# One graph-attention layer: the attention stage in 64-row matmuls, two side by side

## The chip, the core and the metric

The kernel runs on one core of a Trainium2 chip. Its time is the device time in microseconds (us) of that core; of several runs the median counts. In the profile PE is TensorE's matmul side and PEld its weight loads, DVE is VectorE, ACT is ScalarE, POOL is GpSimd and SP is SyncE, which here issues most of the DMAs.

## What is computed

A graph layer over 384 nodes with 1024 features, 16 heads of 64, and a mask from 6528 typed edges. All matrices are 1024 x 1024 in float32.

```python
h = relu(layernorm(x))
q, k, v = h @ wq.T + bq, h @ wk.T + bk, h @ wv.T + bv
q2, k2, v2 = q @ wiq.T + biq, k @ wik.T + bik, v @ wiv.T + biv   # then split into 16 heads of 64
scores = einsum('hnd,hmd->hnm', q2, k2) * 0.125 + mask           # mask from the edges, 384 x 384
out = einsum('hnm,hmd->hnd', softmax(scores), v2)
return x + out @ wo.T + bo
```

## The kernel before, in words

Every factor of a matmul is split into a high part (rounded to the matmul's format) and a low part (the remainder), and a product is three matmuls: high x high, low x high, high x low (`products`, L882 to L886). The high part of anything is made by ScalarE, the low part by VectorE or GpSimd, each behind the other.

The weights come as 56 slabs of 128 x 1024 (512 KB), numbered in the order of use: 0 to 7 v, 8 to 15 the second layer of v, 16 to 23 q, 24 to 31 k, 32 to 47 the second layer of q and k in turns, 48 to 55 the output matrix. SP loads slab s into one of three raw buffers when the low part of slab s - 3 is made. ScalarE makes its high part in one of four ring slots (`split_hi`, L475) when TensorE has used slab s - 4; VectorE makes the low part up to slab 37, GpSimd from slab 38 on (`split_lo`). The last four slabs go into the buffers of q and k, free when all slabs up to 47 are used. A tile is 128 output features by 384 nodes: 24 matmuls, then a move out by ScalarE (`tile_hi_part`) and VectorE (`tile_lo_part`).

The second layer and the attention run interleaved from the tiles of pair 0 on (a pair is two heads, 128 features). Step j = 0 to 8 of the loop over pairs has this order on TensorE (the order is written out by hand, and each engine runs its own list in order):

- `scores(j, n)` for three tiles of 128 nodes: for each of the two heads three matmuls with 64 rows, the heads side by side, into banks 0 to 5;
- `filler(j, 0)`: a second-layer tile, 128 rows (from step 6 on a part of the output product);
- values of the former pair's second head, transposes of the pair before (`turn_pair`: 36 transposes of 64 rows each for a pair, up to pair 5; `turn_probs`: nine of 128x128 for each of the last four heads), and between them the rest of another second-layer tile and `heads_values(h)`: probabilities times v2, 128 rows, six matmuls for each head.

ScalarE's list in a step is: six exponentials with row sums (`exp_part`), slab high parts, tile high part, move of the transposed probabilities (`pt_hi_part`), the half of a head's values that is on the other partitions (`half_part`), and the high part of a finished pair (`pair_hi_part`). VectorE has six maxima with the mask (`max_part`), reciprocals (`inv_part`), low parts of tiles and of transposed probabilities (`pt_lo_part`), and `head_part`, which adds the two halves. In step 0 it also adds the output bias to x (`y_part`). GpSimd normalises (`norm_part`), makes the low parts of slabs and of pairs (`pair_lo_part`). q2 and k2 have two turns each; of the score banks each is used once in a step before transposes take it.

After step 8 the rest of the output product runs in seven pieces, each added to x by VectorE and stored by SP.

Of the kernel before, what the change touches and what calls it, by code (L numbers as in the profile page):

```python
# [20 lines left out]
P = 128  # L21
N = 384
# [26 lines left out]
V0, VV0, Q0, K0, QK0, O0 = 0, KT, 2 * KT, 3 * KT, 4 * KT, 6 * KT  # L49
# [4 lines left out]
TILES_AHEAD = 3  # L54
UNITS_FROM = 2

# [6 lines left out]

LO_ALL = QK0 + TILES_AHEAD + 3

# [5 lines left out]
def gat_kernel(nc, slabs, x, edge_cols, edge_rows, edge_weights, biases, bo, out):  # L71
    with ExitStack() as ctx:
# [3 lines left out]
        def sem(name):  # L76
# [10 lines left out]
        v2 = sb("v2", [P, NT, PAIRS, 4, D], F32R)  # L87
# [5 lines left out]
        q2_hi = sb("q2_hi", [P, 2, N], F32R)  # L93
        q2_lo = sb("q2_lo", [P, 2, N], F32R)
        k2_hi = sb("k2_hi", [P, 2, N], F32R)
        k2_lo = sb("k2_lo", [P, 2, N], F32R)
        work = sb("work", [P, NT * N + N], F32)
        prob = sb("prob", [P, 3, NT, N], F32)
        pt_hi = sb("pt_hi", [P, NT, N], F32R)
        pt_lo = sb("pt_lo", [P, NT, N], F32R)  # L100
        work2 = sb("work2", [P, NT * N + N], F32)
        bias = sb("bias", [P, 6 * KT], F32)
        cols_i = sb("cols_i", [P, 3, ET], I32)
        cols = sb("cols", [P, 2, ET], F32)
        rows_i = sb("rows_i", [ET, 2, P], I32)
        rows = sb("rows", [ET, 2, P], F32)
        key_row = sb("key_row", [ET, P], F32)
# [12 lines left out]
        iota = sb("iota", [P, N], F16)  # L120
# [15 lines left out]
        bo_sb = work2[:, 0:F]  # L136
        head_out = work2[:, NT * N:(NT + 1) * N]
        probs = [[prob[:, 0], prob[:, 1]],
                 [prob[:, 2], work2[:, 0:NT * N].rearrange("p (t n) -> p t n", n=N)]]

        mask_late = prob[:, 1]
        mask_part = prob[:, 0]
# [5 lines left out]
        def key_copy(pos):  # L148

            first, n = [(work2, 0), (work2, 4), (work2, 8), (work, 0), (work, 4), (work, 8), (prob, 19), (prob, 23),  # L150
                        (prob, 3), (prob, 7), (prob, 11), (prob, 15), (prob, 0)][pos], len(tiles_of(UNIT_ORDER[pos])) * P
            flat = prob[:, :, :, :].rearrange("p a t n -> p (a t n)") if first[0] is prob else first[0]
            return flat[:, first[1] * P:first[1] * P + n]
# [10 lines left out]
        pair_bank = bank[6]  # L164
        head_bank = bank[7]
# [53 lines left out]
        def score_bank(c):  # L219

            return bank[c]

        def in_halves(h):

            return h < H - 4

        def pt_place(h, m):

            if not in_halves(h):
                return bank[m][:, 0:N]  # L230
# [945 lines left out]
```

## Time and profile before

| | us |
|---|---|
| median of 3 runs (294.31 to 294.68) | 294.4 |
| span of the profiled execution | 292.6 |
| TensorE busy | 286.9 (98%) |
| VectorE busy | 176.3 (60%) |
| ScalarE busy | 153.7 (53%) |
| GpSimd busy | 149.9 (51%) |

The span is that of one profiled execution; the runs' time has 1.8 us more around it. The chain that ended last runs over TensorE for 96% of the span. The granted TensorE clock is full in all 40 slices. The page's group lines give operation and names, the number of instructions, the busy time and the mean of one, and the idle time ahead of them with what ended it. A matmul's record is longer than the distance to the next start, since matmuls overlap in the pipeline; so work is measured here by start times.

### The profile page before, as it was taken

To read this page: it belongs to the slowest core of one execution; us is meant where nothing else is said; L and a number is where in the kernel's file an instruction comes from. 1 tells how busy PE (TensorE), PEld (TensorE's weight loads), DVE (VectorE), ACT (ScalarE), POOL (GpSimd) and SP (SyncE) were. 2 spreads that over 40 slices of the span, in tenths; PEclk is the share of its full clock that TensorE was granted. 3 is DMA by queue.
4 is the path that set the end of the run, shared out by engine and by line. 5 is a ranking of instruction groups with operands and counts; after the bars stand their busy time and mean duration, and the time that the engine had idled before them with its cause. 6 is when DMAs were issued, how large, how long until landed. Compare 5 with 4: busy or idle time off the path is not lost.

```text
span 292.6 us, 4992 instructions
## 1 busy us (share of the span) xinstructions
PE 286.9 (98%) x1809; PEld 266.0 (91%) x1809; DVE 176.3 (60%) x473; ACT 153.7 (53%) x289; POOL 149.9 (51%) x156
## 2 busy tenths in 40 slices
PE   6999999999999999999999999999999999999996
PEld 3799998888899999999999999999999997888885
DVE  4999878696534543454377676665748475835241
ACT  2986343242542344234434685969687879774100
POOL 6452454453454544644400796748393939873000
PEclk9999999999999999999999999999999999999999
DMA  7969965839643344324454043040403122400032
GB/s 269 324 237 266 330 219 165 249 113 341 222 143 106 112 144 146 116 100 146 164 212 146 0 147 119 26 147 0 146 23 124 50 97 72 146 0 0 2 143 72
DMA packets 15818, 40.84 MB, mean 140 GB/s; under 512 B 3481, under 2 KB 4914, under 8 KB 15794
## 3 DMA queue, kind: packets, MB, share of 16 engines
q1 hardware_dynamic: 13346, 38.53, 39.6%
q0 software_dynamic: 2016, 1.21, 1.5%
q10 hardware_dynamic: 432, 0.79, 0.7%
q8 instruction: 14, 0.23, 0.3%
q14 instruction: 10, 0.08, 0.1%
HBM read 37.71 MB, written 2.81 MB: 138 GB/s over the span
## 4 chain that ended last, share of the span: by engine, by line
PE 96%; DMA 1%; DVE 1%; ACT 0%; POOL 0%; issue 0%
PE banks L884 27%; PE banks L885 26%; PE banks L886 26%; PE banks L1015 5%; PE banks L1058 3%; PE banks L1059 3%; PE banks L1030 3%; PE banks L1043 1%; DMA x_sb<-in_x 1%; PE banks L935 1%; DVE stats L711 1%; PE banks L975 1%; PE banks L965 0%; PE banks L978 0%; ACT x_sb L504 0%; POOL rstd L384 0%
## 5 line engine op out<-in xcount | busy, mean ns | idle before, releaser
L426 POOL DMA_INDIRECT cells<-value,cell x51 | 54.5, 1069 | 60.2 <-DMA cells<-value,cell 47.5
L479 ACT ACTIVATE w_hi<-raw 128x1024 fp32r<-128x1024 f32 x50 | 52.6, 1053 | 19.5 <-PE banks L886 17.3
L886 PE MATMUL banks<-a_lo,w_hi 128*128 128x384 f32 x184 | 61.5, 334 | 0.0
L884 PE MATMUL banks<-a_hi,w_hi 128*128 128x384 f32 x184 | 61.5, 334 | 0.0
L885 PE MATMUL banks<-a_hi,w_lo 128*128 128x384 f32 x184 | 61.5, 334 | 0.0
L747 DVE TENSOR_TENSOR w_lo<-raw,w_hi 128x1024 fp32r<-128x1024 f32 x36 | 44.2, 1229 | 12.4 <-ACT w_hi L479 12.2
L452 POOL TENSOR_SCALAR prob<-prob,row_inv 128x384 f32<-128x384 f32 x36 | 22.6, 645 | 42.6 <-DVE row_inv L814 42.6
L884 PEld LDWEIGHTS banks<-a_hi,w_hi 128*128 128x128 f32 x184 | 34.5, 188 | 0.0
L885 PEld LDWEIGHTS banks<-a_hi,w_lo 128*128 128x128 f32 x184 | 34.5, 188 | 0.0
L886 PEld LDWEIGHTS banks<-a_lo,w_hi 128*128 128x128 f32 x184 | 34.5, 188 | 0.0
L399 POOL TENSOR_TENSOR w_lo<-raw,w_hi 128x1024 fp32r<-128x1024 f32 x14 | 33.7, 2410 | 0.0
L818 DVE TENSOR_TENSOR pt_lo<-banks,pt_hi 128x384 fp32r<-128x384 f32 x48 | 23.8, 551 | 13.3 <-ACT pt_hi L580 13.1
L566 ACT ACTIVATE prob<-prob,neg_max 128x384 f32<-128x384 f32 x36 | 21.8, 606 | 9.2 <-DVE neg_max L804 9.2
L484 ACT ACTIVATE b_hi<-banks,bias 128x384 fp32r<-128x384 f32 x16 | 9.3, 582 | 32.3 <-PE banks L886 32.2
L580 ACT ACTIVATE pt_hi<-banks 128x384 fp32r<-128x384 f32 x48 | 20.1, 490 | 5.7 <-PE banks L1059 4.5
L884 PE MATMUL banks<-c_hi,w_hi 128*128 128x384 f32 x64 | 22.2, 346 | 0.0
L884 PE MATMUL banks<-b_hi,w_hi 128*128 128x384 f32 x64 | 21.9, 343 | 0.0
L735 DVE SCALAR_TENSOR_TENSOR b_lo<-banks,bias,b_hi 128x384 fp32r<-128x384 f32 x16 | 9.9, 616 | 19.7 <-ACT b_hi L484 19.7
L886 PE MATMUL banks<-b_lo,w_hi 128*128 128x384 f32 x64 | 21.4, 335 | 0.0
L885 PE MATMUL banks<-b_hi,w_lo 128*128 128x384 f32 x64 | 21.4, 334 | 0.0
L886 PE MATMUL banks<-c_lo,w_hi 128*128 128x384 f32 x64 | 21.4, 334 | 0.0
L885 PE MATMUL banks<-c_hi,w_lo 128*128 128x384 f32 x64 | 21.4, 334 | 0.0
(151 smaller groups left out, 611.0 us busy)
## 6 DMA issues: line engine op xcount, KB each, us to landing
raw<-in_slabs SPq DMA_DIRECT2D x56, 512.0 KB, 3.4
work<-key_rows SPq DMA_DIRECT2D x6, 256.0 KB, 5.6
prob<-key_rows SPq DMA_DIRECT2D x6, 256.0 KB, 3.9
x_sb<-in_x SPq DMA_DIRECT2D x3, 512.0 KB, 5.2
out_y<-x_sb SPq DMA_DIRECT2D x5, 256.0 KB, 2.1
cells<-prob SPq DMA_DIRECT2D x2, 576.0 KB, 7.6
cells<-value,cell POOLq DMA_INDIRECT x51, 3.7
x_sb<-in_x ACTq DMA_DIRECT2D x3, 256.0 KB, 4.4
```

Source lines behind the costliest of these rows:

```text
L399: nc.gpsimd.tensor_tensor(lo, raw[:, s % RAW, :], hi.bitcast(F32), ALU.subtract).then_inc(slab_lo, 1)
L426: nc.gpsimd.indirect_dma_start(out=cells[c][:, :], out_offset=bass.IndirectOffsetOnAxis(ap=cell[:, t:t + 1], axis=0), in_=value[:, t:t + 1 ...
L452: nc.gpsimd.tensor_scalar(probs[j % 2][x][:, n, :], probs[j % 2][x][:, n, :], row_inv[:, j % 2, c:c + 1], 1.0, ALU.mult, ALU.mult).then_in ...
L479: nc.scalar.activation(split_place(s)[0], raw[:, s % RAW, :], ACT.Copy).then_inc(slab_hi, 1)
L566: nc.scalar.activation(probs[j % 2][x][:, n, :], probs[j % 2][x][:, n, :], ACT.Exp, scale=-1.0, bias=neg_max[:, j % 2, c:c + 1], accum_out ...
L580: nc.scalar.activation(pt_as_placed(pt_hi, h, m), pt_place(h, m), ACT.Copy).then_inc(pt_hi_ok, 1)
L747: nc.vector.tensor_tensor(lo, raw[:, s % RAW, :], hi.bitcast(F32), ALU.subtract).then_inc(slab_lo_dve, 1)
L818: nc.vector.tensor_tensor(pt_as_placed(pt_lo, h, m), pt_place(h, m), pt_as_placed(pt_hi, h, m).bitcast(F32), ALU.subtract).then_inc(pt_lo_ ...
L884: nc.tensor.matmul(psum, w[0], a[0], start=first, stop=False)
L885: nc.tensor.matmul(psum, w[1], a[0], start=False, stop=False)
L886: return nc.tensor.matmul(psum, w[0], a[1], start=False, stop=last)
L1015: mm = nc.tensor.matmul(score_bank(2 * n + x)[:, 0:N], q[own, turn, m], k[own, turn, :], start=(p == 0), stop=(p == 2))
```

## The change

- The whole second layer of q and k and all of attention run in matmuls of 64 rows, two side by side on the two halves of the partitions. Their results go to two banks, so that no sum over both is needed: the upper rows hold q, the lower ones k. For this the tiles of q and k (slabs 16 to 31, now loaded in turns) are written mixed, 64 features of q and 64 of k in each tile, with a bias put together by four small copies (`bias_parts`), and a second-layer slab is read by two transfers of 64 rows, one from q's and one from k's matrix.
- `pair_steps(pair, first, end)` takes the place of `pair_tile`: 48 steps of two matmuls for a pair, cut into pieces between scores, transposes and values.
- Scores of tiles 0 and 2 use banks 0 and 1, those of tile 1 banks 2 and 3. Transposes come in three groups `turn(pair, m)` into banks 2/3, 0/1, 2/3 for both heads and for all pairs; group 2 waits for group 0's low part. They are moved out as 128 x 768 in one operation.
- `pair_values` does both heads, 24 matmuls of 64 rows, into banks 6 and 7.
- q2 and k2 have one turn; both tiles of a pair are moved after the 48 steps, in banks 4 and 5 (pair 1: 6 and 7).
- v2 is kept by blocks of 64 nodes and moved out in four operations of 64 rows for each tile; the second half's first two tiles are moved ahead of the tile of slab 16, the third behind the split of slab 20.
- ScalarE's order in a step is now: pair high part, first slab(s), six exponentials, moves of the transposed probabilities, tiles, second slab(s), halves. Step 7 has slabs 51 and 52 first and 53 second, step 8 slabs 54 and 55 first.
- Output pieces run between the last two pairs and behind them in another order. Small buffers of the start share the memory of the probabilities.

The core of the diff; of the lines taken out none is shown, since they stand in the functions above.

```diff
@@ names and places
+SLABS_OF_STEP = [((37 + 2 * j,), (38 + 2 * j,)) for j in range(PAIRS - 1)] + [((51, 52), (53,)), ((54, 55), ())]
...
+        def score_place(n):
+            return (0, 2, 0)[n]
+        def turn_place(m):
+            return (2, 0, 2)[m]
...
+        def pair_place(pair):
+            return 6 if pair == 1 else 4
...
+            if QK0 <= s < O0:
+                first, half = s - s % 2, slice(s % 2 * D, (s % 2 + 1) * D)
+                return [(raw[rows_of(x)[0], s % RAW, :], slabs[first + x, half, :]) for x in range(2)]
...
@@ ScalarE
+            def v2_hi_part(g, ts):
+                for t in ts:
+                    if t < NT - 1:
+                        act.wait_ge(v2_done, g * (NT - 1) + t + 1)
+                    else:
+                        act.wait_ge(slab_used, VV0 + (g + 1) * KS)
+                    for half in range(2):
+                        for x in range(2):
+                            own, _ = rows_of(x)
+                            nc.scalar.activation(v2[own, 2 * t + half, pairs_of(g), x, :], v2_from(g, t, half, x),
+                                                 ACT.Copy).then_inc(v2_hi, 1)
...
+            def pt_hi_part(pair, m):
+                both = pair * ROW_BLOCKS + 2 * m + 2
+                act.wait_ge(pt_done, both)
+                act.wait_ge(pt_done_high, both)
+                if pair >= 1:
+                    act.wait_ge(head_done, pair)
+                nc.scalar.activation(as_turned_probs(pt_hi, m), turned(m), ACT.Copy).then_inc(pt_hi_ok, 1)
...
+                first, second = SLABS_OF_STEP[j]
+                if 2 <= j < PAIRS:
+                    pair_hi_part(j - 2)
+                for s in first:
+                    split_hi(s)
                 if j < PAIRS:
+                    for n in range(NT):
+                        exp_part(j, n)
                 if j >= 1:
+                    for m in range(2):
+                        pt_hi_part(j - 1, m)
+                if j == PAIRS:
+                    pair_hi_part(PAIRS - 2)
+                if j >= 1:
+                    pt_hi_part(j - 1, 2)
+                if j < PAIRS - 1:
+                    for second_of in range(2):
+                        tile_hi_part(3 * KT + 2 * (j + 1) + second_of)
+                for s in second:
+                    split_hi(s)
+                if j >= 1:
+                    half_part(j - 1)
...
@@ VectorE, the loop over steps
+                    max_part(j, 0)
+                    if j == 0:
+                        y_part(0)
+                    max_part(j, 1)
                     inv_part(j, 0)
+                    if j == 0:
+                        y_part(1)
+                    max_part(j, 2)
                     inv_part(j, 1)
+                    if j == 0:
+                        y_part(2)
                     inv_part(j, 2)
                 if j >= 1:
+                    for m in range(2):
+                        pt_lo_part(j - 1, m)
                 if j == PAIRS:
                     pair_lo_part(PAIRS - 2)
+                if j >= 1:
+                    pt_lo_part(j - 1, 2)
+                if j < PAIRS - 1:
+                    for second_of in range(2):
+                        tile_lo_part(3 * KT + 2 * (j + 1) + second_of)
+                if j >= 1:
+                    head_part(j - 1)
...
@@ TensorE
+            def pair_steps(pair, first, end):
+                if first == 0:
+                    pe.wait_ge(v2_lo, 4 * GS * NT)
+                    if pair >= 1:
+                        pe.wait_ge(tile_lo, 3 * KT + (0, 0, 2, 6)[pair] if pair < 4 else 3 * KT + 2 * pair)
+                for step in range(first, end):
+                    half, k, p = step // STEPS, step % STEPS // 3, step % 3
+                    s, block_at = QK0 + 2 * pair + half, 2 * k + half
+                    if step == first or step % STEPS == 0:
+                        hi, lo = split_slab(s)
+                    if pair == 0 and p == 0:
+                        pe.wait_ge(tile_lo, KT + block_at + 1)
+                    a_h, a_l = (b_hi, b_lo) if block_at < KT else (c_hi, c_lo)
+                    w, a = ((hi, a_h), (lo, a_h), (hi, a_l))[p]
+                    for x in range(2):
+                        own, _ = rows_of(x)
+                        mm = nc.tensor.matmul(bank[pair_place(pair) + x][:, 0:N], w[own, k * P:(k + 1) * P],
+                                              a[own, block_at % KT, :], start=(step == 0), stop=(step == 2 * STEPS - 1))
+                    if step % STEPS == STEPS - 1:
+                        mm.then_inc(slab_used, 1)
...
             def scores(j, n):
+                m, at = slice(n * P, (n + 1) * P), score_place(n)
                 if n == 0:
+                    pe.wait_ge(tile_lo, 3 * KT + 2 * (j + 1))
+                if n == 2:
+                    pe.wait_ge(masked, chunk_at(j, 0, 1) + 1)
+                elif j >= 2:
+                    pe.wait_ge(pt_lo_ok, turn_at(j - 2, n + 1) + 1)
+                elif j == 1:
+                    pe.wait_ge(masked, chunk_at(0, (2, 1)[n], 1) + 1)
...
+            def turn(pair, m):
+                at, j = turn_place(m), pair + 1
+                if m == 0:
+                    pe.wait_ge(prob_ok, chunk_at(pair, NT - 1, 1) + 1)
+                if m == 2:
+                    pe.wait_ge(pt_lo_ok, turn_at(pair, 0) + 1)
+                elif j < PAIRS:
+                    pe.wait_ge(masked, chunk_at(j, m + 1, 1) + 1)
+                else:
+                    pe.wait_ge(pt_lo_ok, turn_at(pair - 1, 2 - m) + 1)
...
+            def pair_values(pair):
+                if pair >= 1:
+                    pe.wait_ge(head_sum, 2 * pair)
+                else:
+                    pe.wait_ge(tile_lo, 3 * KT + 4)
+                order = [(b, p) for b in range(4) for p in range(2)] + [(b, p) for p in range(2) for b in (4, 5)]
+                for i, (b, p) in enumerate(order):
+                    pe.wait_ge((pt_hi_ok, pt_lo_ok)[p], turn_at(pair, b // 2) + 1)
...
+            pair_steps(0, 0, 2 * STEPS)
+            pair_steps(1, 0, FIRST_STEPS)
+            scores(0, 0)
+            pair_steps(1, FIRST_STEPS, 30)
+            scores(0, 1)
+            pair_steps(1, 30, 40)
+            scores(0, 2)
+            pair_steps(1, 40, 48)
+            pair_steps(2, 0, 8)
+            for j in range(1, PAIRS - 1):
+                scores(j, 0)
+                pair_steps(j + 1, 8, 16)
+                scores(j, 1)
+                pair_steps(j + 1, 16, 24)
+                scores(j, 2)
+                pair_steps(j + 1, 24, 32)
+                turn(j - 1, 0)
+                pair_steps(j + 1, 32, 38)
+                turn(j - 1, 1)
+                pair_steps(j + 1, 38, 42)
+                turn(j - 1, 2)
+                pair_steps(j + 1, 42, 48)
+                pair_values(j - 1)
+                if j < PAIRS - 2:
+                    pair_steps(j + 2, 0, 8)
+            last = PAIRS - 1
+            scores(last, 0)
+            scores(last, 1)
+            pe.wait_ge(tile_lo, 5 * KT)
+            out_part(0, range(0, 3))
+            scores(last, 2)
+            turn(last - 1, 0)
+            out_part(1, range(0, 3))
+            turn(last - 1, 1)
+            turn(last - 1, 2)
+            out_part(0, range(3, 5))
+            pair_values(last - 1)
+            turn(last, 0)
+            turn(last, 1)
+            out_part(1, range(3, 5))
+            for n in range(2):
+                out_part(n, range(5, 6))
+            turn(last, 2)
+            for n in range(2):
+                out_part(n, range(6, 7))
+            pair_values(last)
+            out_part(2, range(0, 7))
+            out_part(3, range(0, 7))
+            for piece in range(4):
                 out_part(piece, [KT - 1])
+            for piece in range(4, 7):
+                out_part(piece, range(0, KT))
```

## Rows read from the trace of the kernel before

**Rows 1.** The page, part 1: busy time, share of the span, instructions.

```profile
PE 286.9 (98%) x1809; PEld 266.0 (91%) x1809; DVE 176.3 (60%) x473; ACT 153.7 (53%) x289; POOL 149.9 (51%) x156
```

**Rows 2.** Busy time by stretch, one loop step: stretch, length, then each engine's busy us.

```profile
193.98:207.83 13.85, 13.85 (x117) 13.03 (x116) 8.75 (x28) 10.85 (x25) 9.09 (x9) 1.00 0.25 77
```

**Rows 3.** Order of time, TensorE, one loop step: start us, length us, engine, line, operation.

```profile
193.65 0.34 PE L886 MATMUL banks<-b_lo,w_hi 128*128 128x384 f32 x1
193.91 0.44 PE L1015 MATMUL banks<-k_hi,q_hi 64*128 64x384 f32 x2
194.19 0.34 PE L1015 MATMUL banks<-k_lo,q_hi 64*128 64x384 f32 x2
...
195.41 0.34 PE L1015 MATMUL banks<-k_hi,q_lo 64*128 64x384 f32 x2
195.68 0.44 PE L884 MATMUL banks<-c_hi,w_hi 128*128 128x384 f32 x1
195.96 0.34 PE L885 MATMUL banks<-c_hi,w_lo 128*128 128x384 f32 x1
...
199.78 0.33 PE L886 MATMUL banks<-c_lo,w_hi 128*128 128x384 f32 x1
...
201.09 1.33 PE L1030 MATMUL banks<-ident,prob 64*128 64x64 f32 x36
202.35 0.44 PE L884 MATMUL banks<-b_hi,w_hi 128*128 128x384 f32 x1
202.63 0.34 PE L885 MATMUL banks<-b_hi,w_lo 128*128 128x384 f32 x1
```

**Rows 4.** Order of time, TensorE, steps with the last four heads.

```profile
245.47 0.45 PE L1058 MATMUL banks<-pt_hi,v 128*128 128x384 f32 x1
...
251.77 1.15 PE L1043 MATMUL banks<-ident,prob 128*128 128x128 f32 x9
252.67 0.48 PE L884 MATMUL banks<-w_hi,a_hi 128*128 128x512 f32 x1
252.98 0.39 PE L885 MATMUL banks<-w_hi,a_lo 128*128 128x512 f32 x1
253.21 0.40 PE L886 MATMUL banks<-w_lo,a_hi 128*128 128x512 f32 x1
```

**Rows 5.** Order of time, one tile's last matmul and its two moves, three engines.

```profile
148.36 0.33 PE L886 MATMUL banks<-b_lo,w_hi 128*128 128x384 f32 x1
...
148.73 0.58 ACT L484 ACTIVATE q_hi<-banks,bias 128x384 fp32r<-128x384 f32 x1 [2.63 <-PE banks L886]
...
149.35 0.62 DVE L735 SCALAR_TENSOR_TENSOR q_lo<-banks,bias,q_hi 128x384 fp32r<-128x384 f32 x1 [1.99 <-ACT q_hi L484]
```

**Rows 6.** ScalarE's groups by form (busy, mean ns | idle), then three moves in order of time.

```profile
L479 ACT ACTIVATE w_hi<-raw 128x1024 fp32r<-128x1024 f32 x50 | 52.6, 1053 | 19.5 <-PE banks L886 17.3 <-DMA raw<-in_slabs 2.2
...
L580 ACT ACTIVATE pt_hi<-banks 128x384 fp32r<-128x384 f32 x48 | 20.1, 490 | 5.7 <-PE banks L1059 4.5 <-PE banks L1043 0.9
...
L566 ACT ACTIVATE work<-work,neg_max 128x384 f32<-128x384 f32 x12 | 7.2, 602 | 0.0
L550 ACT ACTIVATE v<-banks 128x512 fp32r<-128x512 f32 x6 | 3.6, 598 | 3.5 <-PE banks L886 3.5
...
201.79 1.26 ACT L580 ACTIVATE pt_hi<-banks 128x384 fp32r<-128x384 f32 x3
```

**Rows 7.** VectorE's groups by form, then three moves in order of time.

```profile
L818 DVE TENSOR_TENSOR pt_lo<-banks,pt_hi 128x384 fp32r<-128x384 f32 x48 | 23.8, 551 | 13.3 <-ACT pt_hi L580 13.1
...
L787 DVE TENSOR_TENSOR v<-banks,v 128x512 fp32r<-128x512 f32 x6 | 3.9, 686 | 1.0 <-ACT v L550 1.0
...
L833 DVE TENSOR_TENSOR x_sb<-x_sb,work 128x1024 f32<-128x1024 f32 x3 | 3.9, 1299 | 0.0
...
202.39 1.49 DVE L818 TENSOR_TENSOR pt_lo<-banks,pt_hi 128x384 fp32r<-128x384 f32 x3
```

**Rows 8.** GpSimd's group by form: low parts of slabs.

```profile
L399 POOL TENSOR_TENSOR w_lo<-raw,w_hi 128x1024 fp32r<-128x1024 f32 x14 | 33.7, 2410 | 0.0
```

More of the change, by code:

```diff
@@ L61 @@
 assert 2 * CHAIN == NT + ET and LATE == 6 * EG and sorted(UNIT_ORDER) == list(range(GROUPS))
-LO_ALL = QK0 + TILES_AHEAD + 3
+LO_ALL = QK0 + 2 + AHEAD
+SLABS_OF_STEP = [((37 + 2 * j,), (38 + 2 * j,)) for j in range(PAIRS - 1)] + [((51, 52), (53,)), ((54, 55), ())]
+assert [s for step in SLABS_OF_STEP for part in step for s in part] == list(range(LO_ALL, SLABS))
 def tiles_of(group):
@@ L250, in split_place, with loads_through, raw_place @@
+        def loads_through(s):
+            return sum(len(slab_loads(r)) for r in range(s % RAW, s + 1, RAW))
+        def raw_place(s):
+            if Q0 <= s < QK0:
+                return raw[:, s % RAW, :].rearrange("p (k a d) -> p a k d", a=2, d=D)
+            return raw[:, s % RAW, :]
         def split_place(s):
             j = s - O0 - KS
+            if Q0 <= s < QK0:
+                first = (s - s % 2) % RING
+                return tuple(a[:, first:first + 2, :].rearrange("p a (k x d) -> p a k x d", x=2, d=D)[:, :, :, s % 2, :]
+                             for a in (w_hi, w_lo))
@@ L294, in rows_of @@
             return slice(own, own + D), slice(D - own, 2 * D - own)
-        assert [s for j in range(PAIRS) for part in slabs_of_step(j) for s in part] == list(
-            range(QK0 + TILES_AHEAD + AHEAD, SLABS))
         @block.sync
@@ L317, in _ @@
                     sp_eng.wait_ge(x_in[0][0], 16)
-                sp_eng.dma_start(raw[:, s % RAW, :], slabs[s]).then_inc(slab_in[s % RAW], 16)
+                for into, source in slab_loads(s):
+                    sp_eng.dma_start(into, source).then_inc(slab_in[s % RAW], 16)
                 if s == 1:
@@ L526, in _ @@
             act.wait_ge(small_in, 16)
-            for s in range(QK0 + TILES_AHEAD):
+            for s in range(QK0 + 2):
                 if s < 2:
                     tile_hi_part(s)
+                if Q0 <= s < QK0 and s % 2 == 1:
+                    tile_hi_part(s - KT)
                 split_hi(s + AHEAD)
@@ new lines, in _ @@
+            for j in range(PAIRS + 1):
+                first, second = SLABS_OF_STEP[j]
+                if 2 <= j < PAIRS:
+                    pair_hi_part(j - 2)
+                for s in first:
+                    split_hi(s)
+                if j < PAIRS:
+                    for n in range(NT):
+                        exp_part(j, n)
+                if j >= 1:
+                    for m in range(2):
[11 more added lines that the diff above has]
+                    half_part(j - 1)
@@ L764, in _ @@
                 split_lo(s)
-            for s in range(QK0 + TILES_AHEAD):
+            for s in range(QK0 + 2):
                 if s < 2:
                     tile_lo_part(s)
+                if Q0 <= s < QK0 and s % 2 == 1:
+                    tile_lo_part(s - KT)
                 if lo_by_vector(s + AHEAD):
@@ L1014, in scores @@
                         own, _ = rows_of(x)
-                        mm = nc.tensor.matmul(score_bank(2 * n + x)[:, 0:N], q[own, turn, m], k[own, turn, :],
+                        mm = nc.tensor.matmul(bank[at + x][:, 0:N], q[own, m], k[own, :],
                                               start=(p == 0), stop=(p == 2))
```

489 lines of the change are left out of this document (174 added, 315 removed).

## The prediction

> **What bounds the kernel now.** I read the page's first part, then the table by stage, then the order of time on TensorE around one loop step. TensorE is busy for 286.9 of the 292.6 us of the profiled span [rows 1], and in the loop step from 193.98 to 207.83 for all of 13.85 us, while VectorE needs 8.75, ScalarE 10.85 and GpSimd 9.09 [rows 2]. So the sum is TensorE's work plus whatever waits it gets. Busy is not useful, though. Matmuls of 384 columns start 0.1735 us apart (22 intervals between 195.96 and 199.78), and two 64-row matmuls side by side count as one start with 0.174 us to the next (seven intervals from 194.19 to 195.41) [rows 3]. Where the height changes, from 128 rows to 64, the starts are 0.26 and 0.28 us apart (193.65, 193.91, 194.19); going back, 0.27 or 0.28 us (195.68, 195.96). Out of the 36 transposes it is the same: 202.35 to 202.63 [rows 3]. That is about 0.09 before and 0.10 us after each change. The step checks it: 69 starts by 0.1735 are 11.97, 36 transposes are 1.26 less 0.09 = 1.17, and four changes of height have the rest, 13.85 - 13.14 = 0.71, or 0.175 each.
>
> **What the change takes from TensorE.** Changes of height: before there are two in step 0, four in each of steps 1 to 6 and two in step 7, 28 in all. After, one leads into the second layer, and eleven lie around the output pieces put between the last two pairs: 12. 16 fewer by 0.175 are -2.8 us. Transposes of the last four heads: nine of 128x128 take 0.90 us (251.77 to 252.67), and the matmul behind them runs 0.31 instead of 0.23 us [rows 4], 0.98 for each head, 3.9 for four. The same four heads as 72 small ones at 1.17/36 = 0.0325 cost 2.35 us: -1.6 us. Second layer: 384 full matmuls become 384 pairs, and values 96 full ones become 96 pairs, at 0.174 against 0.1735: between 0 and +0.2; I take 0.
>
> **What it adds there.** Each pair's transposes now come in three groups with matmuls between. Even without a change of height the first matmul after transposes stands 0.08 us longer [rows 4]. Three groups in six steps are 18 returns: between 0 (the small ones may leave room to load weights) and +1.8 (with 0.02 going in as well). I take +1.4, since rows 4 has exactly this passage. Work alone: -2.8 - 1.6 + 1.4 = -3.0 us. Before has three short waits in the values of step 6 (one record at 245.47 is 0.45 instead of 0.33 us [rows 4]); I count 0.3 for them, gone: -3.3 us. Without new waits that would be 294.4 - 3.3 = 291.1.
>
> **A rule of the skill.** On two 64-row matmuls for one of 128 rows the rows show no cost. The Trainium skill ("TensorEngine Tiling (Array Packing)", Instruction Overhead) gives each matmul an overhead of some 60 cycles. By it the 480 additional matmuls would cost 60 cycles of 2.4 GHz each, an estimate of 12 us and a time near 306; the trace disagrees as far as nine pairs in a row can tell.
>
> **What other engines need.** New buffers are tighter: q2 and k2 have one turn, scores and transposed probabilities share banks 0 to 3, and TensorE waits for their moves. An engine starts about 0.20 us after TensorE's slot ends (matmul at 148.36, slot to 148.53, ScalarE at 148.73), and VectorE 0.04 after ScalarE (0.58 from 148.73, then 149.35) [rows 5]. ScalarE's operations start 0.1 us before the former's record ends (three take 1.26 instead of 3 x 0.49) [rows 6], VectorE's 0.08 (three in 1.49) [rows 7]. The move of transposes is now 768 wide. No row has that; from 0.490 at 384 and 0.598 at 512 on ScalarE [rows 6] I extend to 0.81, from 0.551 and 0.686 on VectorE to 0.95 [rows 7]. Bounds: one fixed part less than two old ones (0.7 and 0.9) and two old ones (0.98 and 1.10). Moves of v in four parts of 256 fall in ScalarE's and VectorE's idle time before the second layer; TensorE next asks for them many microseconds later. Slabs of two 64-row transfers: 16 more issues on SP's queue, with a slab wanted every 6 to 7 us (two in a step) and each slot of the raw ring free a whole slab earlier; 0, and +0.5 at most. In the stage of q and k the ring frees two slots at once and refills them in some 4.2 of 8.3 us: 0.
>
> **A middle step, walked** (0 = scores of tile 0). TensorE: scores 1 ends at 2.4, scores 2 at 4.3, transposes 0 at 6.1, 1 at 7.6, 2 should start at 8.4, pair j+1 is complete at 9.9, values until 12.0, next step at 13.4. ScalarE: the last two exponentials wait for the maxima of scores 2 and run from 5.13 by 0.60 each [rows 6], so move 0 runs 6.33 to 7.14 and VectorE's part to 8.1: in time by 0.2. The tiles of pair j+1 are moved from 10.1 (ScalarE) to 11.9 (VectorE, 0.62 each, behind the last move of transposes); TensorE wants their banks at 12.0. No wait, with under 0.1 us in hand.
>
> **The first step.** VectorE now adds the output bias between the maxima, three operations of 1.3 us [rows 7]. With 0 at the second layer's start: scores 2 end at 17.0, maxima to 18.2, the third addition to about 19.7, then the two tiles of pair 1 to 21.0. Scores of step 1 want them at 19.8. In before the tiles were moved a step earlier. A wait of +1.0 to +1.2; I take +1.0. Between 0 and 1.4.
>
> **The last steps** (0 = scores of pair 7, which follow the values of pair 5 directly, with no filler). ScalarE's queue: both halves of values 5 to 1.3, the head to 2.3 (VectorE's sums between), slabs 51 and 52 to 4.2 (0.94 each, from 1.053) [rows 6], six exponentials to 7.8, only then move 0 of pair 6, to 8.6; VectorE to 9.6. TensorE stands before transposes 2 of pair 6 at 7.2, as they take the bank of transposes 0: wait 2.4 us. Then values 6 end at 13.9. ScalarE: their halves to 15.1, slabs 54 and 55 to 16.9, move 0 of pair 7 to 17.7, VectorE to 18.7; TensorE wants to go on at 17.7: wait 1.1. The head of pair 6 is next in that queue, its low part ready at 20.1, and the output parts of k = 6 want it at 19.3: wait 0.9. GpSimd, with two slabs of 2.41 us [rows 8] and six normalisations, is ready at 11.6 for a need at 13.9. Each wait has 0.1 more for the late weight load. Together +4.4 + 0.3. Before had one half-head at a time in that queue and output work between, with scarcely a wait there.
>
> **Sum.** -3.3 + 1.0 + 4.7 = +2.4 us. If the returns from transposes cost nothing, it would be +1.0, or 295.4. The profiled span of 292.6 and the median of 294.4 differ by 1.8 us around the span; I leave that as it is: 296.8 us.
>
> **Rivals.**
> (a) TensorE's work alone sets the time: the waits of the last steps are covered, because the exponentials of pair 7 are done by the time the transposes want ScalarE. For it: the changes of height are certain to go; ScalarE is idle for 3.0 us of a step of before [rows 2]. Against it: the fixed order of ScalarE's queue. 291.1 without any wait, 292.1 with the first step's; I take 292.1 as its time. 0.22.
> (b) Half the waits: 294.4 - 3.3 + 2.9 = 294.0, a draw, up to 295.0. 0.13.
> (c) Middle steps wait too: the moves cost what two old ones did, 0.17 and 0.15 more than I take, three times in a chain which has under 0.2 us of room. It decides from a move of 0.9 us on. Some 0.3 us in each of six steps, +1.8: 298.6. 0.11.
> (d) The pairs are slower in long runs than nine in a row: at 0.01 us each (records of 0.34 instead of 0.33 stand in rows 3) for 480 pairs, +4.8: 301.6. By the rule above it would be more. 0.04.
> The forecast itself, 295 to 298.5, has 0.50.
>
> **How the numbers follow.** A measurement of this kernel tells 0.2%, some 0.6 us, from no change. Slower: forecast, (c), (d): 0.65. Within: (b), 0.13. Faster: (a), 0.22. The range 291.0 to 298.8 leaves out (d), a part of (c) and the case where the transposes' returns cost nothing and no wait comes.
>
> **What would show it.** In the profile after: middle steps of about 13.4 us instead of 13.85 with no changes of height; pairs every 0.174 us; TensorE idle (or its weight loads) waiting for VectorE's low part of the transposed probabilities in the last steps, once for over 2 us; 1 us before the scores of pair 1; moves of 768 at 0.81 and 0.95 us. The prediction is wrong if no idle time of over 1 us stands in the last 45 us, if middle steps take 13.8 or more, or if pairs in long runs are not at 0.174.

## The result, and the profile after

| | before | after |
|---|---|---|
| median, side by side | 294.53 us (4 runs, 294.31 to 294.68) | 300.62 us (4 runs, 299.82 to 302.42) |
| ratio | | 1.0216 (1.0181 to 1.0251) |
| profiled execution | span 292.6 us | 299.9 us, span 298.2 us |
| TensorE busy | 286.9 us [rows 1] | 286.0 us |
| a middle step | 13.85 us [rows 2] | 13.40 us |

The changed kernel is slower by 6.1 us, clear of noise. The sign was forecast, the size was not: 2.4 us, with a range that ended at 298.8. The profiled span is longer by 5.6 us, and that difference is explained below.

The page after, its span, busy times, TensorE's slices and the granted clock in the 40 slices:

```profile
span 298.2 us, 5957 instructions
PE 286.0 (96%) x2325; PEld 266.7 (89%) x2325; DVE 179.3 (60%) x442; ACT 159.4 (53%) x287; POOL 153.4 (51%) x157
PE   6999999999999999999999899999999998959996
PEclk9999999999999999999999999999999999799999
```

Against [rows 1] TensorE has 0.9 us less to show. Three slices of 7.5 us that were full are not: an 8 around 168 us, where the scores of pair 1 wait, and an 8 and a 5 near the end. One slice, the 35th (253.5 to 260.9 us), has a clock of 7. There was nothing of that in before.

The page's groups of the two moves of transposed probabilities, now 768 wide:

```profile
L891 DVE TENSOR_TENSOR pt_lo<-banks,pt_hi 128x768 fp32r<-128x768 f32 x24 | 22.8, 956 | 11.1 <-ACT pt_hi L653 11.1
L653 ACT ACTIVATE pt_hi<-banks 128x768 fp32r<-128x768 f32 x24 | 19.2, 810 | 7.5 <-PE banks L1113 7.5
```

A middle step (scores of tile 0 to the next scores of tile 0), and the stretch from the scores of pair 7 to transposes 2 of pair 6. Columns: stretch, length, busy us of PE, PEld, DVE, ACT, POOL with counts, granted clock, DMA share, GB/s:

```profile
178.88:192.28 13.40, 13.40 (x178) 13.21 (x177) 8.49 (x23) 10.85 (x22) 9.21 (x10) 1.00 0.29 81
244.40:254.19 9.79, 7.56 (x64) 5.62 (x61) 5.56 (x19) 8.70 (x20) 9.56 (x7) 1.00 0.38 116
```

The next one takes 13.42 us. The middle steps have the length that was worked out, and TensorE is busy in all of it. So the loss lies at the first step and at the last two. The same view in stretches of 2 us:

```profile
252.00:254.00 2.00, 0.00 (x0) 0.00 (x0) 0.99 (x2) 1.84 (x4) 2.00 (x4) 1.00 0.84 254
254.00:256.00 2.00, 1.81 (x17) 1.57 (x18) 1.26 (x3) 1.11 (x2) 2.00 (x4) 0.94 0.64 240
256.00:258.00 2.00, 2.00 (x10) 1.35 (x11) 0.70 (x1) 0.66 (x1) 1.42 (x2) 0.50 0.00 0
258.00:260.00 2.00, 2.00 (x20) 1.99 (x18) 0.00 (x0) 0.00 (x0) 1.10 (x1) 0.71 0.00 0
```

Here is what the prediction didn't have. TensorE stands for 252 to 254. It works again, and from 256 to 258 it is granted 0.50 of its speed, that is 1.2 GHz instead of 2.4; the neighbouring stretches have parts of it. A clock of c over t us gives up t times (1 - c): 0.12 + 1.00 + 0.58 = 1.7 us. A "busy" of 2.00 hides this, and the clock's column shows it.

TensorE in order of time over the last steps (start, length, the wait before it in brackets with its releaser):

```profile
254.19 0.59 PE L1113 MATMUL banks<-ident,prob 64*128 64x64 f32 x12 [2.23 <-DVE pt_lo L891]
...
255.51 0.41 PE L945 MATMUL banks<-w_hi,a_hi 128*128 128x512 f32 x1
255.74 0.61 PE L946 MATMUL banks<-w_hi,a_lo 128*128 128x512 f32 x1
256.14 0.63 PE L947 MATMUL banks<-w_lo,a_hi 128*128 128x512 f32 x1
...
257.51 0.52 PE L1129 MATMUL banks<-pt_hi,v 64*128 64x384 f32 x2
257.83 0.52 PE L1129 MATMUL banks<-pt_lo,v 64*128 64x384 f32 x2
...
265.18 0.58 PE L1113 MATMUL banks<-ident,prob 64*128 64x64 f32 x12 [1.28 <-DVE pt_lo L891]
267.73 0.50 PE L945 MATMUL banks<-w_hi,a_hi 128*128 128x512 f32 x1 [1.97 <-DVE a_lo L810]
```

Three waits stand where three were predicted, with the releasers that were named. The lower clock is in the starts too: 0.23 us from 255.51 to 255.74 for 512 columns, 0.40 to 256.14, and pairs 0.32 apart instead of 0.174. The last wait, 1.97 instead of 0.9 us, has its reason on two other engines. VectorE and then GpSimd, in order of time:

```profile
264.17 1.82 DVE L891 TENSOR_TENSOR pt_lo<-banks,pt_hi 128x768 fp32r<-128x768 f32 x2 [2.17 <-ACT pt_hi L653]
265.90 1.77 DVE L810 TENSOR_TENSOR a_lo<-spare,a_hi 128x384 fp32r<-128x384 f32 x1
```

```profile
264.90 2.36 POOL L456 TENSOR_TENSOR c_lo<-raw,c_hi 128x1024 fp32r<-128x1024 f32 x1
```

A 384-wide subtraction takes VectorE 1.77 us here. GpSimd's slab runs until 267.26, and VectorE's operation ends 0.41 us after it.

**Where the 5.6 us of the profiled span are.** The walk of the prediction puts the first output matmul of k = 6 at 20.2 us after the scores of pair 7 (need at 19.3, ready at 20.1, and 0.1). It stands at 267.73 - 244.40 = 23.3. Of these 3.1 us, 1.7 are the clock and 1.2 VectorE's long subtraction (1.77 - 0.56), with 0.2 left. The predicted +2.4 and these 3.1 are 5.5 of the 5.6 us. The trace by itself gives a second account. The four waits are 0.87 + 2.23 + 1.28 + 1.97 = 6.35 us. Take 1.2 of them for the long subtraction, and 5.15 are left where the prediction had 5.4. With the 1.7 of the clock this leaves 298.2 - 6.35 - 1.7 = 290.15 for TensorE's work, 2.5 less than before, where the prediction had 3.0 less (3.3, less the 0.3 for late weight loads). These two small errors cancel in part.

### The profile page after: what moved, and what is told of

Its sections match the earlier page's. It is cut to its first block and busy times, and to the rows that moved or that the text cites. A ratio compares the mean times of both kernels' runs of the same rounds, so it can differ in the third digit from the quotient of the medians.

```text
span 298.2 us, 5957 instructions
## 1 busy us (share of the span) xinstructions
PE 286.0 (96%) x2325; PEld 266.7 (89%) x2325; DVE 179.3 (60%) x442; ACT 159.4 (53%) x287; POOL 153.4 (51%) x157
## 5 line engine op out<-in xcount | busy, mean ns | idle before, releaser
L877 DVE CUSTOM_DVE_ANT_0 prob<-banks,work 128x384 f32<-128x384 f32 x48 | 24.8, 555 | 14.2 <-PE banks L1091 14.1
L891 DVE TENSOR_TENSOR pt_lo<-banks,pt_hi 128x768 fp32r<-128x768 f32 x24 | 22.8, 956 | 11.1 <-ACT pt_hi L653 11.1
L1072 PE MATMUL banks<-c_lo,w_hi 64*128 64x384 f32 x128 | 23.8, 340 | 0.0
L1072 PE MATMUL banks<-c_hi,w_hi 64*128 64x384 f32 x128 | 23.8, 340 | 0.0
L1072 PE MATMUL banks<-b_lo,w_hi 64*128 64x384 f32 x128 | 23.7, 340 | 0.0
L1072 PE MATMUL banks<-b_hi,w_hi 64*128 64x384 f32 x128 | 23.6, 341 | 0.0
L1072 PE MATMUL banks<-c_hi,w_lo 64*128 64x384 f32 x128 | 23.3, 331 | 0.0
L653 ACT ACTIVATE pt_hi<-banks 128x768 fp32r<-128x768 f32 x24 | 19.2, 810 | 7.5 <-PE banks L1113 7.5
L1072 PE MATMUL banks<-b_hi,w_lo 64*128 64x384 f32 x128 | 23.2, 332 | 0.0
L947 PE MATMUL banks<-w_lo,b_hi 128*128 128x512 f32 x48 | 18.7, 389 | 0.0
```

Source lines behind the costliest of these rows:

```text
L877: nc.vector.tensor_tensor_reduce(out=prob_chunk(j, n, x), in0=in_blocks(bank[score_place(n) + x][:, 0:N]), in1=in_blocks(mask[:, n, :]), s ...
L891: nc.vector.tensor_tensor(as_turned_probs(pt_lo, m), turned(m), as_turned_probs(pt_hi, m).bitcast(F32), ALU.subtract).then_inc(pt_lo_ok, 1)
L947: return nc.tensor.matmul(psum, w[0], a[1], start=False, stop=last)
L1072: mm = nc.tensor.matmul(bank[pair_place(pair) + x][:, 0:N], w[own, k * P:(k + 1) * P], a[own, block_at % KT, :], start=(step == 0), stop=( ...
```

## The experiments

After's extra time was put down at first to two causes besides the waits that were predicted: the clock that falls behind the first wait, and GpSimd's slab that holds up VectorE. The rivals were that all of it is the waits, that the bias additions cost the first step, and that pairs or heights cost something in long runs. The slabs' low parts on GpSimd, the order of ScalarE's queue and TensorE's own order were changed one by one. In e1, e8 and e9 TensorE does extra matmuls whose sums are overwritten by the ones that follow: these kernels do more work than after, never less.

**e1: work in the first wait.** 13 pairs of 64-row matmuls before transposes 2 of pair 6.

```diff
+            def hold(pairs, pair):
+                pe.wait_ge(head_sum, 2 * pair)
+                for _ in range(pairs):
+                    for x in range(2):
+                        own, _ = rows_of(x)
+                        nc.tensor.matmul(head_bank[x][:, 0:N], a_hi[own, KT - 1, 0:P], a_hi[own, KT - 1, :],
+                                         start=True, stop=True)
...
             turn(last - 1, 1)
+            hold(13, last - 1)
             turn(last - 1, 2)
```

> The changed kernel with 13 pairs of 64-row matmuls (a_hi times a_hi into the two idle head banks, overwritten later) put between transposes 1 and 2 of pair 6, where TensorE idled for 2.2 us. They add 13 x 0.174 = 2.3 us of work inside the wait. Theory A (the wait lets the granted clock fall to its lower level from 255.7 us on, which costs another 2 us): the clock stays at its upper level behind the wait, transposes 2 still start when VectorE's low part is there, the stretch behind is 2.0 us shorter: 298.6 us against 300.6. Theory B (the clock would have fallen anyway, or the wait alone costs): no gain, 300.6, and the lower clock still stands in the rows.

Measured: 300.38 us (299.86 to 300.94), before beside it 294.34, ratio 1.0210 (1.0191 to 1.0228). Nothing gained. TensorE's waits of e1, and its stretches further on:

```profile
263.64 0.59 PE L1113 MATMUL banks<-ident,prob 64*128 64x64 f32 x12 [1.31 <-DVE pt_lo L891]
266.19 0.50 PE L945 MATMUL banks<-w_hi,a_hi 128*128 128x512 f32 x1 [1.96 <-DVE a_lo L810]
```

```profile
256.00:258.00 2.00, 2.00 (x22) 1.73 (x22) 0.69 (x1) 0.65 (x1) 1.38 (x2) 1.00 0.02 6
...
266.00:268.00 2.00, 1.81 (x5) 1.48 (x6) 1.00 (x2) 0.00 (x0) 0.00 (x0) 0.64 0.00 0
268.00:270.00 2.00, 2.00 (x10) 1.35 (x11) 0.00 (x0) 0.00 (x0) 0.00 (x0) 0.50 0.00 0
```

The expectation was right about the clock behind this wait and wrong about the sum. With the first wait filled the clock stays at 1.00 in 256 to 258, and the transposes of pair 7 come at 263.64 instead of 265.18. But the two waits that are left are followed by a fall in their turn, at 266 to 270: 0.72 + 1.00 = 1.7 us. In this execution the loss was moved, not taken away.

**e2: ScalarE's exponentials ahead of its slabs.** Only the order of slabs in the last two steps. ScalarE and GpSimd both go by this list, so both queues change.

```diff
-SLABS_OF_STEP = [((37 + 2 * j,), (38 + 2 * j,)) for j in range(PAIRS - 1)] + [((51, 52), (53,)), ((54, 55), ())]
+SLABS_OF_STEP = [((37 + 2 * j,), (38 + 2 * j,)) for j in range(PAIRS - 1)] + [((), (51, 52, 53)), ((), (54, 55))]
```

> The changed kernel with slabs 51 and 52 moved behind the exponentials and moves of step 7, and 54 and 55 behind the moves of step 8 (ScalarE's and GpSimd's lists). If ScalarE's queue sets the waits of the last steps: the wait before transposes 2 of pair 6 falls from 2.2 to about 0.6 us, that before transposes 2 of pair 7 (1.3) goes, the clock does not fall (2.0), and a wait for the low part of pair 6 remains, since GpSimd still works on a slab then: 5 to 5.6 us less in all, 295.0 to 295.6. If slabs or their loads set them: the waits only change places, 299 or more.

Measured: 294.81 us (10 runs, 294.51 to 295.82), ratio 1.0017 (1.0007 to 1.0027), mean clock 0.999 or 1.0 in all ten. TensorE's two waits over 0.1 us that are left in the last steps, then VectorE's subtraction, then GpSimd beside it:

```profile
252.69 0.58 PE L1113 MATMUL banks<-ident,prob 64*128 64x64 f32 x12 [0.53 <-DVE pt_lo L891]
262.80 0.50 PE L945 MATMUL banks<-w_hi,a_hi 128*128 128x512 f32 x1 [1.43 <-DVE a_lo L810]
```

```profile
261.01 1.73 DVE L810 TENSOR_TENSOR a_lo<-spare,a_hi 128x384 fp32r<-128x384 f32 x1
```

```profile
257.59 4.74 POOL L456 TENSOR_TENSOR b_lo<-raw,b_hi 128x1024 fp32r<-128x1024 f32 x2
```

One line of order is worth 5.8 us. ScalarE's rows in after have the two slabs first, then the six exponentials from 248.76 on, then moves 0 and 1 of pair 6:

```profile
246.86 1.05 ACT L530 ACTIVATE w_hi<-raw 128x1024 fp32r<-128x1024 f32 x1
247.81 1.04 ACT L530 ACTIVATE b_hi<-raw 128x1024 fp32r<-128x1024 f32 x1
...
252.35 1.48 ACT L653 ACTIVATE pt_hi<-banks 128x768 fp32r<-128x768 f32 x2
```

In e2 the exponentials start at 247.24 and the first move at 250.86. The cause of the waits that was predicted, ScalarE's fixed queue with slabs ahead of the exponentials, is shown: 2.23 becomes 0.53, 1.28 is gone and 1.97 becomes 1.43. That is 3.5 us, and some 2 us of clock come on top. With no wait of about 2 us the clock stays. The long subtraction is still there, beside another slab of GpSimd's.

**e3: the third bias addition later.** VectorE's `y_part(2)` behind the two tiles of pair 1.

```diff
                     max_part(j, 2)
                     inv_part(j, 1)
-                    if j == 0:
-                        y_part(2)
...
                         tile_lo_part(3 * KT + 2 * (j + 1) + second_of)
+                if j == 0:
+                    y_part(2)
```

> The changed kernel with VectorE's third addition of the output bias moved behind the low parts of pair 1's tiles in step 0. If that addition is what the scores of pair 1 wait for: the wait of 0.9 us before them goes, 299.6. If ScalarE's chain is (exponentials, then the tiles' high parts): 0.3 or less is gained, 300.3.

Measured: 300.66 us (299.91 to 302.26), ratio 1.0229 (1.0192 to 1.0265). Nothing gained: the wait before the scores of pair 1 is 0.87 as in after. So the third addition, which the prediction had in this chain, does not set the wait, and the expectation's second theory, ScalarE's chain, holds. TensorE's wait in after, VectorE around it, and ScalarE's first move behind the exponentials, whose last starts at 162.96:

```profile
165.36 0.44 PE L1091 MATMUL banks<-k_hi,q_hi 64*128 64x384 f32 x2 [0.87 <-DVE k_lo L794]
```

```profile
162.78 1.20 DVE L907 TENSOR_TENSOR x_sb<-x_sb,prob 128x1024 f32<-128x1024 f32 x1
...
164.16 0.62 DVE L794 SCALAR_TENSOR_TENSOR q_lo<-banks,bias,q_hi 128x384 fp32r<-128x384 f32 x1
164.69 0.61 DVE L794 SCALAR_TENSOR_TENSOR k_lo<-banks,bias,k_hi 128x384 fp32r<-128x384 f32 x1
```

```profile
163.56 0.56 ACT L537 ACTIVATE q_hi<-banks,bias 128x384 fp32r<-128x384 f32 x1
```

The addition ends at 163.98, but `q_lo` needs `q_hi`, which ends at 164.12 on ScalarE behind the exponentials. Two chains end within 0.14 us of each other; taking away one leaves the other. In e3, with the addition gone, VectorE stands idle for `q_hi`:

```profile
164.38 0.62 DVE L794 SCALAR_TENSOR_TENSOR q_lo<-banks,bias,q_hi 128x384 fp32r<-128x384 f32 x1 [0.30 <-ACT q_hi L537]
```

The releaser named by the profile is the last link only.

**e4: GpSimd's last slabs after VectorE's subtraction.** One wait in GpSimd's queue, ahead of its slabs of the last step.

```diff
                     pair_lo_part(j - 2)
+                if j == PAIRS:
+                    pool.wait_ge(head_lo, PAIRS - 1)
                 for s in first:
                     split_lo(s)
```

> The changed kernel with GpSimd's low parts of slabs 54 and 55 started only when VectorE has made the low part of pair 6. That operation took 1.77 us beside GpSimd's slab and 0.56 at the end of before, where GpSimd was idle. If GpSimd's reads hold it up: it takes 0.56 and the output parts of k = 6 start 1.2 us earlier, 299.4. If it is slow for itself (place, operands, PSUM order): 1.77 again and no gain, 300.6.

Measured: 297.88 us (297.01, 297.21, 298.55, 299.97 with mean clocks of 1.0, 0.998, 0.994 and 0.988), ratio 1.014 (1.0094 to 1.0185). VectorE, TensorE's first wait, then a stretch behind it, of the profiled execution:

```profile
264.46 0.55 DVE L812 TENSOR_TENSOR a_lo<-spare,a_hi 128x384 fp32r<-128x384 f32 x1
```

```profile
254.29 0.59 PE L1115 MATMUL banks<-ident,prob 64*128 64x64 f32 x12 [2.25 <-DVE pt_lo L893]
```

```profile
256.00:258.00 2.00, 2.00 (x20) 1.64 (x21) 0.79 (x1) 0.75 (x1) 1.38 (x2) 1.00 0.03 8
```

The subtraction takes 0.55 instead of 1.77 us with GpSimd idle, so the hold-up is shown, at 1.2 us. The Trainium skill ("SBUF — State Buffer", Who interferes with whom) says that a VectorE instruction with two inputs in SBUF contends with a GpSimd instruction that reads SBUF, that the port pair they share is an exclusive lock, and that the order of issue decides which of the two is blocked. The trace agrees: 1.77 us beside the slab that had begun first, 0.55 without. The trace of before had a milder case, a subtraction of the same kind that took 0.83 us and ended 0.41 us after GpSimd's slab; VectorE, then GpSimd, of before:

```profile
265.86 0.83 DVE L740 TENSOR_TENSOR a_lo<-work,a_hi 128x384 fp32r<-128x384 f32 x1
```

```profile
263.88 2.40 POOL L399 TENSOR_TENSOR c_lo<-raw,c_hi 128x1024 fp32r<-128x1024 f32 x1
```

The second thing was not expected. After a wait as long as after's the clock stays up in this execution, and the time, 297.21, is 2.7 us under after's 299.9: 1.2 for the subtraction and 1.5 for the clock. The other three have no trace, only time and mean clock: 297.01 at 1.0, 298.55 at 0.994 and 299.97 at 0.988. A fall of 1.7 us is 0.6% of the span, so these read as no fall, one and two. So the same waits bring the clock down in some executions of one kernel and not in others.

**e5: both.** The order of e2 with one slab fewer in the step of pair 7, and GpSimd's wait ahead of the last slabs.

```diff
+SLABS_OF_STEP = [((37 + 2 * j,), (38 + 2 * j,)) for j in range(PAIRS - 1)] + [((), (51, 52)), ((), (53, 54, 55))]
...
+                if j == PAIRS:
+                    pool.wait_ge(head_lo, PAIRS - 1)
                 for s in second:
                     split_lo(s)
```

> As e2_order, with slab 53 too moved behind the moves of step 8, and GpSimd's three last slabs started only when VectorE has made the low part of pair 6. If GpSimd's reads held VectorE up in e2_order (1.73 us for that operation): it takes 0.56 us again, and the wait of 1.43 us before the output parts of k = 6 falls to about 0.3: 293.6 us against 294.8. If not: 294.8.

Measured: 293.65 us (9 runs, 293.36 to 294.45), ratio 0.9969 (0.9948 to 0.9991): 1.2 under e2. The subtraction takes 0.55 us (at 260.59), and TensorE's wait for it is down from e2's 1.43 to 0.17.

**e6: more work ahead of the scores of pair 1.** e5, with six steps of pair 2 moved there.

```diff
             pair_steps(1, 40, 48)
-            pair_steps(2, 0, 8)
+            pair_steps(2, 0, 14)
...
-                pair_steps(j + 1, 8, 16)
+                pair_steps(j + 1, 14 if j == 1 else 8, 16)
```

> As e5_order_gpsimd, with six more pairs-steps of pair 2 (1.04 us of work that has to be done anyway) ahead of the first scores of step 1, taken out behind them. If the 0.87 us wait there is the distance from pair 1's last matmul to its use (two moves by ScalarE and VectorE behind exponentials): the wait goes, 292.7. If it moves to the next scores: no gain, 293.6.

Measured: 292.46 us (292.36 to 293.04), ratio 0.9941 (0.9924 to 0.9957). The scores of pair 1 start at 165.23 with no wait, though six more pairs (1.04 us) stand ahead of them than in after, where they start at 165.36. The gain over e5 is 1.2 us, for a wait of 0.87 and the late first matmuls behind it. With e3 this settles the first step: what counts is how much work of TensorE's lies between pair 1's last matmul and its first use, not the third addition on VectorE.

**e7: output work between the transposes of pair 6.** e6 with `out_part(0, range(3, 5))` ahead of `turn(last - 1, 2)`.

> As e6_first_step, with the two output parts that stood behind transposes 2 of pair 6 moved ahead of them, where 0.5 us of wait was left; the count of changes of height stays. If that wait is covered by them and nothing behind becomes late: 292.2. If pair 6's third move is now late for its values: 292.7 or more.

Measured: 292.39 us (292.36 to 292.76), ratio 0.9936 (0.9919 to 0.9953). No gain over e6. The trace of e6 has two waits in the last steps, 0.53 us before transposes 2 of pair 6 (251.30) and 0.19 before k = 6 (260.20). In e7 they are 0.18 us in the values of pair 6 (254.93) and 0.41 before k = 6 (260.19): the same matmul starts at the same time, as it is VectorE's chain to the low part of pair 6 that sets it.

**e8: changes of height put back.** e7, and one 128-row matmul ahead of the values in five of the middle steps.

```diff
+                if 1 <= pair <= 5:
+                    nc.tensor.matmul(head_bank[0][:, 0:N], a_hi[:, KT - 1, 0:P], a_hi[:, KT - 1, :],
+                                     start=True, stop=True)
                 order = [(b, p) for b in range(4) for p in range(2)] + [(b, p) for p in range(2) for b in (4, 5)]
```

> As e7_output_between, with one 128-row matmul of 384 columns (its result is overwritten) ahead of the values in each of steps 2 to 6. If a change of height costs 0.175 us as read from before: five times 0.17 for the work and 0.35 for going there and back, +2.6 us, steps of 13.9 instead of 13.4. If heights are free and only the work counts: +0.9.

Measured: 294.77 us (10 runs, 294.63 to 295.12), 2.4 over e7. TensorE of e8 around one of them:

```profile
201.56 0.34 PE L1074 MATMUL banks<-c_lo,w_hi 64*128 64x384 f32 x2
201.83 0.44 PE L1126 MATMUL banks<-a_hi 128*128 128x384 f32 x1
202.20 0.45 PE L1134 MATMUL banks<-pt_hi,v 64*128 64x384 f32 x2
202.48 0.34 PE L1134 MATMUL banks<-pt_lo,v 64*128 64x384 f32 x2
```

Each costs 0.48 us, of which 0.17 is its own work: 0.155 for a change of height. In the trace the three intervals take 0.92 us where two would take 0.35, and with 0.17 for the matmul itself 0.20 is left for a change. The two figures differ because something else gets shorter. Behind the values of a middle step the last two pairs and the first pair of the next work take 0.42 and 0.25 us in e7 (starts at 202.74, 203.16 and 203.41), instead of 0.35 and 0.17. In e8 they take 0.35 and 0.17 (204.06, 204.41, 204.58). So the 0.155 is a net figure. The 0.175 of the prediction lies between, and the theory by which a change costs nothing, +0.9 in all, falls.

**e9 and e10: what the clock costs.** After with all three waits filled: e1's 13 pairs, seven before transposes 2 of pair 7 and ten before k = 6; beside it, on the same chip, after again, unchanged.

```diff
+            hold(7, last)
             turn(last, 2)
+            hold(10, last)
             for n in range(2):
                 out_part(n, range(6, 7))
```

> The changed kernel with side work in all three long waits of the last steps: 13 pairs as in e1_fill, 7 before and 10 behind transposes 2 of pair 7 (results overwritten). No wait gets shorter in itself. Theory A (waits let the clock fall, in e1_fill the fall only moved to the next wait): the granted clock stays at its upper level throughout, 298.2 us, and the executions lie as close together as those of before (0.5 us instead of 2.6). Theory B (the clock falls whatever TensorE does here): 300 us or more, wide spread.

> The changed kernel as it is, beside e9_fill_all on the same chip: 300.6 us with executions between 299.8 and 302.4 and a granted clock of 0.988 to 0.994, if the loss to the lower clock differs from execution to execution; the waits themselves should be the same in each.

Measured: e9 298.56 us (298.45 to 299.01), ratio 1.014 (1.0123 to 1.0157); e10 300.62 us (299.76 to 301.56), ratio 1.0201 (1.0173 to 1.0230). In e9 the granted clock is 1.00 all the way from 254 to 274. Stretches of e10:

```profile
254.00:256.00 2.00, 1.68 (x16) 1.41 (x17) 1.25 (x3) 0.97 (x2) 2.00 (x5) 0.89 0.70 244
256.00:258.00 2.00, 2.00 (x9) 1.25 (x10) 0.84 (x1) 0.79 (x1) 1.41 (x2) 0.50 0.03 8
258.00:260.00 2.00, 2.00 (x22) 2.00 (x19) 0.00 (x0) 0.00 (x0) 1.24 (x1) 0.76 0.00 0
...
268.00:270.00 2.00, 2.00 (x8) 1.28 (x10) 0.70 (x1) 0.00 (x0) 0.00 (x0) 0.80 0.00 0
270.00:272.00 2.00, 2.00 (x14) 2.00 (x14) 0.00 (x0) 0.00 (x0) 0.00 (x0) 0.50 0.00 0
```

e9 does 30 pairs more than e10 and is 2.06 us faster, with a mean clock of 0.999 or 1.0 in all four executions. The profiled execution of e10 has two falls, each of 1.7 us by its stretches (0.22 + 1.00 + 0.48, and 0.40 + 1.00 + 0.32 with 272 to 274 at 0.84). So after has two times: 299.8 to 299.9 with one fall (mean clock 0.993 or 0.994) and 301.3 to 302.4 with two (0.988 or 0.989), and a median between. The number of falls is seen in the two profiled executions; in the others it is inferred from the mean clock.

## Why the prediction was right in sign and wrong in size

- **Changes of height, 0.175 us each.** Right: the traces have 28 changes in before and 12 in after from the second layer on, and e8 gives 0.155 to 0.20.
- **Returns from transposes, +1.4.** The amount came out and the reason did not, which is luck. The middle step is 0.26 us longer than its 69 pairs and 36 transposes, as the sum had it with three returns of 0.08. But twelve transposes (0.39) and the pair behind them (0.174) take 0.59 us, so a return costs some 0.03. The other 0.15 stands behind the values, where two pairs take 0.42 and the next one 0.25 us. The prediction had no such term, and no run isolates its cause.

```profile
184.60 0.52 PE L1113 MATMUL banks<-ident,prob 64*128 64x64 f32 x11
...
185.19 0.39 PE L1072 MATMUL banks<-b_hi,w_hi 64*128 64x384 f32 x2
...
190.39 0.56 PE L1129 MATMUL banks<-pt_lo,v 64*128 64x384 f32 x4
190.81 0.44 PE L1072 MATMUL banks<-b_hi,w_hi 64*128 64x384 f32 x2
191.06 0.37 PE L1072 MATMUL banks<-b_hi,w_lo 64*128 64x384 f32 x2
```

- **Pairs at 0.174 us.** Right in long runs as in short ones. The six intervals from 144.91 to 145.95 near the start of the second layer are 0.173 each. The rival by which pairs cost 0.01 us more each falls with the middle steps, which are as long as worked out without it. Read as an addition to each matmul, the overhead that the Trainium skill ("TensorEngine Tiling (Array Packing)", Instruction Overhead) states would have made each of the eight steps about 1.5 us longer, an eighth of the estimate of 12; the trace disagrees. The section also says that a matmul of one column takes as long as one of 60, and read as such a floor it adds nothing at 384 columns, which fits the trace.
- **TensorE's work alone, 291.1 us.** Nearly: e6 has 0.72 us of waits left in the last steps and 292.46, so 291.7. Some of the 0.6 stands ahead of the second layer, whose first matmul comes at 144.62 instead of 144.37 with 0.09 for its change of height.

- **Moves of 768 columns.** Right: 810 and 956 ns for 0.81 and 0.95. Rival (c), middle steps that wait, didn't come; ScalarE's 0.81 does not reach its point of decision, 0.9 us.
- **The first step, +1.0.** The size was right (0.87 and a late start), the cause was not: the third addition does not decide (e3), the distance does (e6).
- **The last steps, three waits of 2.4, 1.1 and 0.9.** The first two were right, at 2.23 and 1.28, with 9.79 us for a walked 9.6, and the cause was right (e2). Rivals (a) and (b), waits covered or halved, fall.
- **The step that failed** is the sum of these last steps, "Together +4.4 + 0.3": it adds waits as if TensorE came out of each at full speed, and takes the low part of pair 6 to be ready at 20.1 with its undisturbed length. The clock was not priced: 1.7 us for a fall in the profiled execution, 2.1 between the medians of e9 and e10. The hold-up by GpSimd was not priced: 1.2 us (e4, e5). The prediction walked GpSimd's queue only for its own readiness, and not for who runs beside it, though before's subtraction of 0.83 us was there to be read. 296.8 + 2.1 + 1.2 = 300.1 of 300.62. The 0.5 left is about the 0.6 by which TensorE's work alone was too low; what makes up the rest of that is open.
- **The range.** Its upper end, 298.8, came from cases of +0.3 us per step and the like. It had no case for what a wait does to the work behind it; in before TensorE never waited long enough here to show one. A wait forecast at 2.4 us in a kernel with none should have widened it by itself.

The small matmuls themselves do not cost the 6 us; the queues around them do. With the slabs' order, GpSimd's wait and the longer lead into pair 1 (e6) the same small matmuls give 292.46 us, and e7 292.39, both 0.6 to 0.7% ahead of before's 294.44 beside them. Before was not given these reorderings, so its best time isn't known.

## What to carry to other kernels

When a change makes an order tighter, walk the fixed queues of the engines that feed the busy one: here two slabs of 0.94 us ahead of six exponentials, and two more ahead of the next moves, were worth 5.8 us with the clock, and one line put it right. Price a new wait of about 2 us on TensorE with more than its length, since the work behind it may run at half the clock (1.7 us here), and read the clock's column before believing a busy share of 1.00. For each VectorE operation with two operands in SBUF on the path, look at what GpSimd runs at that moment.

## What the hardware showed beyond what was expected

- After TensorE stood for 2.23 us the granted clock went from 2.4 to 1.2 GHz about 1.5 us into the following work, and was back some 3.4 us later: 1.7 us lost. The fall is not certain: with a wait of the same cause, place and length it didn't come in the profiled execution of e4. In that of e10 a second one followed the last waits. Falls are part of why the times of one kernel differ: 2.6 us in after (299.82 to 302.42) against 0.6 in e9, whose waits are filled but for 0.21 us. Not every difference is a fall, though. Executions of before beside e5 to e10 took 296.7 to 296.9 us at a mean clock of 0.999 or 1.0 (three of 26), and one beside e1 had a mean of 0.95 at the usual 294.61; nothing here shows why.
- The Trainium skill ("TensorE: Matmul & The Clock Gate", HAM oscillation — how this bites in real kernels) tells of waits for DMA, longer than these, behind which TensorE's clock falls every time. The trace agrees that a wait can bring the clock down, and shows more: a single one of 2.2 us can do it, and only in some executions of one kernel (e4).
- The last two waits are the same in after, e1 and e10 (1.28 to 1.32 and 1.96 or 1.97 us). A fall follows them in the profiled executions of e1 and e10, and none in after's or e3's. What decides is open.
- A GpSimd slab lengthened a VectorE subtraction of 0.55 us to 1.77, 1.73 and 1.83 us (after, e2, e9), and in each it ended 0.41 us after the slab.
- The first pair of 64-row matmuls behind small transposes cost some 0.03 us more than one in a run; behind nine 128x128 transposes the same return was 0.08 us [rows 4].
